# A two-layer transformer kernel: the rotary stage in batches, maxima on 32 rows with one set of keys, and five plus four maxima ahead of the first scores

## What is computed

```python
scores = einsum('bhqd,bhkd->bhqk', q, k) * 64 ** -0.5 + causal     # layer 0, head dimension 64
out = softmax(scores) @ v
...
q = rmsnorm(apply_rope(q, cos, sin), qn_w)                         # layer 1, head dimension 8
k = rmsnorm(apply_rope(k, cos, sin), kn_w)
attn = softmax(where(causal, einsum('bthd,bshd->bhts', q, k) / sqrt(8), -inf))
```

## Time and profile before

| | |
|---|---|
| runs | 1468.04 us median of 3 (1463.27 to 1469.57) |
| profiled execution, own time | 1474.87 us, span 1473.2 us |
| mean granted TensorE clock | 0.897 of full speed |
| PE busy | 1256.4 us, 85% |
| DVE busy | 982.3 us, 67% |
| ACT busy | 691.6 us, 47% |
| POOL busy | 381.6 us, 26% |
| layer 0 attention | about 39 to 590 us of the span |
| rotary stage | 925 to 960.6 us |
| layer 1 attention | 960.7 to 1276 us |

### The profile page before, as it was taken

The page is one execution under the profiler, slowest core; times in us unless marked ns, Lnnn a source line. Parts: engine busy times, 40 slices in busy tenths (PEclk is TensorE's granted clock), DMA queues, the critical chain, the costliest instruction groups (busy, mean ns, idle before and its releaser), DMA issues. The chain is left out here.

```text
span 1473.2 us, 20295 instructions
## 1 busy us (share of the span) xinstructions
PE 1256.4 (85%) x7132; PEld 758.2 (51%) x7132; DVE 982.3 (67%) x1750; ACT 691.6 (47%) x1319; POOL 381.6 (26%) x243
## 2 busy tenths in 40 slices
PE   4679999999999999589999976257988888789997
PEld 3444554545455454358888755123433343257886
DVE  4557646565755542579999956757677665448998
ACT  2232534444352434336666645213566557425664
POOL 0035465646656568000000000301111111020000
PEclk9799999999999999669999968657999979868999
DMA  3101202111120200046767400141222201111221
GB/s 107 42 15 36 50 16 60 24 50 30 39 44 16 46 16 29 4 97 148 156 147 158 96 1 0 15 115 30 49 62 61 53 20 35 29 43 60 96 90 29
DMA packets 51472, 81.54 MB, mean 55 GB/s; under 512 B 16749, under 2 KB 34453, under 8 KB 47445
## 3 DMA queue, kind: packets, MB, share of 16 engines
q1 hardware_dynamic: 51004, 79.40, 22.1%
q10 hardware_dynamic: 384, 1.05, 0.6%
HBM read 63.75 MB, written 5.68 MB: 47 GB/s over the span
## 5 line engine op out<-in xcount | busy, mean ns | idle before, releaser
L1369 PE MATMUL ps<-qA 128*128 128x512 f32 x960 | 254.1, 402 | 10.4 <-POOL qA L1479 10.4
L640 DVE TENSOR_REDUCE mraw<-ps 128x1 f32<-128x512 f32 (+3 forms) x304 | 183.2, 654 | 72.7 <-PE ps L520 41.3
L743 ACT ACTIVATE shared<-ps 128x512 f32<-128x512 f32 (+1 forms) x216 | 118.8, 565 | 227.5 <-PE ps L553 221.5
L1086 DVE TENSOR_REDUCE mraw<-ps 128x2 f32<-128x1024 f32 (+3 forms) x160 | 173.5, 1114 | 71.0 <-PE ps L994 47.8
L1141 ACT ACTIVATE shared<-ps 128x512 f32<-128x512 f32 (+2 forms) x320 | 154.7, 560 | 130.1 <-PE ps L1010 129.9
L1369 PEld LDWEIGHTS ps<-qA 128*128 128x128 f32 x960 | 183.5, 194 | 60.0 <-POOL qA L1479 12.1
L552 PE MATMUL ps<-qA,kH 128*128 128x512 f32 (+3 forms) x384 | 164.5, 438 | 8.2 <-DMA qB<-mT 6.5
L781 POOL TENSOR_TENSOR VP<-VP,shared 128x2048 f32<-128x2048 f32 (+3 forms) x40 | 129.7, 3242 | 66.1 <-ACT shared L743 64.0
L1433 ACT CAST qA<-shared 128x512 fp32r<-128x512 f32 x160 | 99.3, 620 | 87.3 <-DVE shared L1571 86.4
L1381 PE MATMUL ps<-qA,kH 128*128 128x512 f32 x480 | 135.5, 391 | 4.1 <-DVE qA L1495 4.0
L514 PE MATMUL ps<-kH,qA 128*128 128x512 f32 (+3 forms) x384 | 121.0, 380 | 17.1 <-DVE qA L630 8.9
(11 more groups left out here) (250 smaller groups left out, 1890.9 us busy)
## 6 DMA issues: line engine op xcount, KB each, us to landing
shared<-comb SPq DMA_DIRECT2D x92, 256.0 KB, 4.2
qB<-qA SPq DMA_DIRECT2D x16, 512.0 KB, 4.8
rB<-a0rec_dram SPq DMA_DIRECT2D x60, 128.0 KB, 2.9
shared<-comb SPq DMA_DIRECT2D x7, 1024.0 KB, 4.4
rB<-a1rec_dram SPq DMA_DIRECT2D x28, 128.0 KB, 2.7
e0wUp<-in_w SPq DMA_DIRECT2D x48, 64.0 KB, 4.6
qA<-q_split SPq DMA_DIRECT2D x24, 128.0 KB
q_split<-qA SPq DMA_DIRECT2D x4, 512.0 KB
```

The costliest lines, as they stand in the source:

```text
L640: nc.vector.tensor_reduce(out[:, h0:h0 + n_h, qt % 4], src, AX, ALU.max).then_inc(w_free, 1)
L743: nc.scalar.activation(probs(n)[:, hs[0]:hs[-1] + 1, lo:512], src, ACT.Exp, scale=scale)\
L1086: nc.vector.tensor_reduce(out[:, :, js[0]:js[-1] + 1, qt % 4], src, AX, ALU.max).then_inc(x_free, 1)
L1369: ins = nc.tensor.matmul(bank[0:M, :], w[par][:, at:at + M], h[:, cols], start=(r == 0), stop=(r == 2))
```

## The change

1. `stage_attention64`: the 3 projections and the first 2 maxima of qc = 1 of group 0 go ahead of unit 0, behind the first turn. 25 maxima and the turn stay in units 0 to 3.
2. `stage_attention8`: `step_of` puts 11 jobs ahead of unit 0 (first turn and then 4 maxima of qc = 1) and 22 into units 0 to 3.
3. `stage_attention8`: the maxima's matmuls read 32 rows (`TERMS`) of queries and keys, so row 32 doesn't enter. One key set is left. Masks and scores stay on 64 rows. A load has 8 transfers where it had 12, the direct loads 12 for a batch where they had 16 (`LOADS`, `DIRECT`), and two stacks less are cleared.
4. `stage_rope`: VectorE's and ScalarE's orders are written out: batch 0 goes through square, root and scaling while batch 1 is rotated between, the split of chunks 0 and 1 comes ahead of the scaling of batch 1, and ScalarE issues `direct_keys` ahead of the split of chunks 2 and 3.

```diff
-    plan = {-1: jobs_of(0, 0)}
-    spread_over(jobs_of(0, 1), 0, 4)
+    ahead = jobs_of(0, 1)
+    plan = {-1: jobs_of(0, 0) + ahead[0:U + 2]}
+    spread_over(ahead[U + 2:], 0, 4)
...
+    AHEAD = BEFORE + 4
...
-        if idx < BEFORE:
+        if idx < AHEAD:
             return -1
         if idx < EARLY:
-            return (idx - BEFORE) * 4 // (EARLY - BEFORE)
+            return (idx - AHEAD) * 4 // (EARLY - AHEAD)
...
-        DIRECT, LOADS, STORES = 16, 12, 8
+        DIRECT, LOADS, STORES = 12, 8, 8
...
-                            rows = row_tile(i, 64)
+                            rows = row_tile(i, TERMS)
                             ins = nc.tensor.matmul(pair[:, i, slot * w:(slot + 1) * w],
                                                    Q[g % 3][rows, jj, qt * P:(qt + 1) * P],
-                                                   kZero[g % 3][rows, ch * 512:ch * 512 + w],
+                                                   K[g % 3][rows, ch * 512:ch * 512 + w],
...
-                            for dst in (kZero, kOne):
-                                sp.dma_start(dst[g % 3][at:at + 2 * hd, :].bitcast(F32), src)\
-                                    .then_inc(in_ld[g % 3], 16)
+                            sp.dma_start(K[g % 3][at:at + 2 * hd, :].bitcast(F32), src).then_inc(in_ld[g % 3], 16)
...
+                first, second = rotation(0), rotation(1)
+                for _ in first:
+                    pass
+                next(second)
+                squares(0)
+                next(second)
+                scaled(0)
+                next(second)
+                lows_of(0)
+                squares(1)
+                lows_of(1)
+                scaled(1)
+                lows_of(2)
+                lows_of(3)
...
+                squared(0)
+                deviation(0)
+                highs_of(0)
+                squared(1)
+                highs_of(1)
+                deviation(1)
                 act.wait_ge(padded, 2)
                 act.wait_ge(low, 2 * CPB)
                 direct_keys(act, k, 0)
+                highs_of(2)
+                highs_of(3)
...
-                for stack in (k.kL[0], k.kL[1], k.kH[0], k.kH[1]):
+                for stack in (k.kH[0], k.kH[1]):
```

More of the change, by code:

```diff
@@ L942, in stage_attention8 @@
         LAST = slice(P - REP * hd, P)
-        Q, kZero, kOne = split_buffers(k)
+        Q, K = split_buffers(k)
         def landed(g):
@@ L1010, in score_job @@
                         ins = nc.tensor.matmul(score_bank(s)[:, slot * w:(slot + 1) * w],
-                                               kOne[g % 3][rows, kt * P:(kt + 1) * P],
+                                               K[g % 3][rows, kt * P:(kt + 1) * P],
                                                Q[g % 3][rows, h // 2, qc * 512 + lo:(qc + 1) * 512],
@@ L1154, in _ @@
                         for at in (TERMS, 64 + TERMS):
-                            ins = nc.gpsimd.memset(kOne[2][at:at + 1, :].bitcast(F32), 1.0)
+                            ins = nc.gpsimd.memset(K[2][at:at + 1, :].bitcast(F32), 1.0)
                         ins.then_inc(cleared, 1)
@@ L1700, in split_buffers @@
     Q = [k.qA[0][:, 0:2, :], k.qA[0][:, 2:4, :], k.qA[1][:, 0:2, :]]
-    kZero = [k.kL[0][:, :], k.kL[1][:, :], k.qA[1][:, 2, :]]
-    kOne = [k.kH[0][:, :], k.kH[1][:, :], k.qA[1][:, 3, :]]
-    return Q, kZero, kOne
+    K = [k.kH[0][:, :], k.kH[1][:, :], k.qA[1][:, 3, :]]
+    return Q, K
 def direct_queries(engine, k, b):
@@ L1727, in direct_keys @@
             at = 64 * i + 2 * hd * part
-            for sets in split_buffers(k)[1:]:
-                engine.dma_start(sets[b][at:at + 2 * hd, :].bitcast(F32), src).then_inc(k.a1_in[b], 16)
+            engine.dma_start(split_buffers(k)[1][b][at:at + 2 * hd, :].bitcast(F32), src).then_inc(k.a1_in[b], 16)
 def stage_rope(nc, k, qkv, sel8):
@@ L1758, in link, with rotation @@
                     dve.wait_ge(chain, n[0])
-                for b in range(B):
+                def rotation(b):
                     x = qkv[:, tiles(b), 0:HQK * hd].rearrange("p t (h e) -> p t h e", h=HQK)
@@ L1767, in _, with squares @@
                     link(nc.vector.tensor_tensor(o[:, :, :, hi], x[:, :, :, lo], sin, ALU.mult))
+                    yield
                     link(nc.vector.tensor_tensor(s[:, :, :, lo], x[:, :, :, hi], sin, ALU.mult))
+                    yield
                     link(nc.vector.tensor_tensor(s[:, :, :, hi], x[:, :, :, hi], cos, ALU.mult))
                     link(nc.vector.tensor_tensor(o[:, :, :, lo], o[:, :, :, lo], s[:, :, :, lo], ALU.subtract))
-                    roped = nc.vector.tensor_tensor(o[:, :, :, hi], o[:, :, :, hi], s[:, :, :, hi], ALU.add)
-                    roped.then_inc(rotated, 1)
-                for b in range(B):
+                    nc.vector.tensor_tensor(o[:, :, :, hi], o[:, :, :, hi], s[:, :, :, hi], ALU.add)\
+                        .then_inc(rotated, 1)
+                    yield
+                def squares(b):
                     dve.wait_ge(sq_ready, b + 1)
@@ L1778, in _, with scaled @@
                                             ALU.add).then_inc(var_ready, 1)
-                for b in range(B):
+                def scaled(b):
                     dve.wait_ge(std_ready, b + 1)
@@ L1784, in _, with lows_of @@
                                             ALU.mult).then_inc(ready, 1)
-                for ch in range(NC):
+                def lows_of(ch):
                     cols = slice(ch * 512, (ch + 1) * 512)
@@ L1799, in _, with highs_of @@
                 nc.scalar.copy(k.VP[:, :, :, 0:hd], qkv[:, :, HQK * hd:].rearrange("p t (v e) -> p t v e", v=NKV))
[L1800 to L1806, removed]
+                def highs_of(ch):
                     cols = slice(ch * 512, (ch + 1) * 512)
@@ L1811, in _, with squared, deviation @@
                                          scale=k.col("k_w")[0:32, :]).then_inc(high, 1)
+                def squared(b):
+                    act.wait_ge(rotated, b + 1)
+                    nc.scalar.activation(sq[:, tiles(b), :], r[:, tiles(b), :], ACT.Square).then_inc(sq_ready, 1)
+                def deviation(b):
+                    act.wait_ge(var_ready, b + 1)
+                    nc.scalar.activation(ms[:, 1, heads(b)], ms[:, 0, heads(b)], ACT.Sqrt).then_inc(std_ready, 1)
+                squared(0)
[4 more added lines that the diff above has]
+                deviation(1)
                 act.wait_ge(padded, 2)
```

## The result

The changed kernel takes 1544.09 us, the median of 4 runs (1541.27 to 1564.84), against 1465.72 us for the kernel before (1463.27 to 1469.57): a ratio of 1.0526, 95% interval 1.0488 to 1.0564. The forecast was 1452 in a range of 1436 to 1470. It is wrong in sign and by 92 us; not even rival A (1485) comes near.

What follows compares the result with a forecast made beforehand. VectorE and transfers were taken to bound the starts, TensorE (88% busy) layer 1's steady part; -6.5 - 6 - 4 - 2.5 - 11 + 14 = -16 us from 1468.0 gave 1452 us, range 1436 to 1470.

Steps and rivals of the forecast that it cites:

- rival A: Mode changes decide: 263 drains at 0.14 us, no overlap, more gaps lowering the clock; +17 us, 1485 us; chance 0.14.
- Part 1: Layer 0's attention: projections and maxima ahead start the first maximum 7.2 us earlier and unit 4 6.5 us earlier.
- Part 2: Rotary stage and direct loads: earlier scaling and 12 transfers for batch 0 bring layer 1's first scores 6 us earlier.
- Part 3: Layer 1's units 0 to 3: four maxima leave VectorE's chain, 4 us; a small copy avoids GpSimd's clearing, 2.5 us.
- Part 4: Layer 1's loads without the second key set: 7 us fewer TensorE waits, 4 us less lower clock, together 11 us.
- rival B: Mode changes cost nothing, 32 rows being handled as 64-row halves: -30 us, 1438 us; chance 0.15.
- Part 5: TensorE's changes between matmul shapes: 263 more at 0.093 us, plus lost overlap; price taken as 14 us, bounds 0 and 31.
- the second piece that the prediction named: On TensorE, a maximum can no longer overlap with the score in the other row half: up to 10 us more.
- The test that the prediction set itself: TensorE's group time, about 31 us: over 34 means mode changes cost more than taken, below 29 hidden or absent.

Runs made afterwards that it cites:

- the kernel on 64 rows: Changed kernel with only the maxima's matmuls put back on 64 rows, still one key set: 1433.51 us, ratio 0.9758 to the kernel before.
- the kernel with two key sets: Changed kernel with two key sets and maxima on 64 rows as before, its other edits kept: 1454.72 us, ratio 0.9906 to the kernel before.
- the kernel with 32 rows from group 3 on: Changed kernel with maxima on 64 rows up to group 2 and on 32 rows from group 3: 1498.09 us, ratio 1.0014 to the kernel before.
- all on 32 rows: Changed kernel with scores and masks cut to 32 rows like the maxima: 1535.23 us, ratio 1.0457 to the kernel before.

## Why the prediction was wrong

**Right, with sizes** (parts as the prediction numbers them). Part 1: first scores at 60.4 (59.5 forecast), unit 4 at 84.3 (85). Part 2: first maximum 33.1 us behind the start of the rotary stage (33), first scores 46.1 (47). Part 3: the copy at 0.17 us (0.2), and in the kernel with these four maxima alone 9.3 us less from the first scores to the end of group 0, rather than 6.5. Part 4: in the kernel on 64 rows `recips` waits 1.63 us at most up to 1200 us (1.7), and the waits for maxima shrink to 0.9 us. Six groups shorten by 10.7 against the kernel with two key sets, where the sum had 11. All gains together were forecast as 30 and measured as 36.0 (interval 29.5 to 41.6): that is the kernel on 64 rows, and rival B's 1438 was its time but for 5 us, though not its cause: that kernel has no changes of mode between 32 and 64 rows.

**Part 5, what a change of mode takes, was right too.** Time from the start of one pair of 512 columns to the next pair, where TensorE waits for nobody, medians (those of the changed kernel at the full clock rest on 5 to 8 places): score to maximum 0.337 us without a change (kernel on 64 rows) and 0.433 with one (changed kernel), both at the full clock: 0.096, forecast 0.093. Maximum to score 0.233 and 0.430: 0.197. That is more than the 0.096; the rest would be the second piece that the prediction named, a score that no longer overlaps with the maximum, but no run separates the two. At the lower clock score to maximum is 0.594 and 0.724. Such rows of the changed kernel at the full clock:

```profile
1230.59 0.51 PE L1012 MATMUL ps<-qA 64*128 64x512 f32 x2
1231.03 0.49 PE L985 MATMUL ps<-kH,qA 32*128 32x512 f32 x2
1231.45 0.88 PE L1012 MATMUL ps<-qA 64*128 64x512 f32 x2
```

and at the lower:

```profile
1152.75 0.79 PE L1012 MATMUL ps<-qA,kH 64*128 64x512 f32 x2
1153.48 0.80 PE L985 MATMUL ps<-kH,qA 32*128 32x512 f32 x2
1154.20 0.88 PE L1012 MATMUL ps<-qA,kH 64*128 64x512 f32 x2
```

Most of it is hidden: the group between 1131.8 and 1163.5 us of the kernel with 32 rows from group 3 on, wholly at 1.00, takes 31.7 us, a group on 64 rows 30.4 (182.7 / 6). That is 1.3 a group, or 2.0 against the same group on 64 rows (29.7): some 10 to 16 for eight, where 14 was taken, from a single group. At 0.50 it is 3.8 a group (49.7, the mean of the changed kernel's groups 1 to 3, against 45.9 all on 32 rows).

**The step that failed** is the sum's silent term: the prediction let the clock follow the idle time of TensorE alone. Under part 4 it took 4 us off because fewer gaps would mean less time at 0.50, and under part 5 it charged a 32-row matmul its late start and its lost overlap, and nothing for how the clock would take fewer rows. At 1.00 all 8 groups would have cost some 10 to 16 us more than on 64 rows, an estimate of 1444 to 1450 us for the whole. The other 94 to 100 are the clock: a group takes 46 us all on 32 rows at 0.50 where it takes 30.4 on 64 rows at 1.00, and the changed kernel spent 325 of the 373 us from 960 to 1333 at 0.50. Rival A had the lower clock as a result of more gaps; there were fewer gaps. Nor does a run show the drain of 0.14 us at each change that this rival counts with; measured is the later start, 0.096 us from score to maximum and 0.197 from maximum to score at the full clock. In the 110 us from 1090 on TensorE idles 1.9, in the 182.7 of the 64-row kernel 18.9, and it is the first that stays at 0.50.

The test that the prediction set itself pointed the right way and named the wrong cause: groups of over 34 us were to mean that changes of mode cost more. Four of the six took 49 to 51, with each change at the price taken.

The clock didn't follow TensorE's busy share: it is busy 237.6 of 246.7 us at 0.50 in the changed kernel and 163.8 of 182.7 at 0.99 with maxima on 64 rows. In these kernels the clock went by how many rows the matmuls read as well.

**Open.** How the level depends on rows between 33, 48 and 64, on columns, and why scores and maxima on 32 rows don't weigh quite alike. What starts a fall is open too: some come behind a turn's idle time and some behind none, and no kernel moved the turns.

## What to carry to other kernels

A matmul that reads fewer rows wasn't cheaper on TensorE here (0.427 us from a maximum to the next score at 0.50, all on 32 rows or all on 64), and where such matmuls filled much of the time the engine stayed at half its clock for 247 us on end while it looked 96% busy. Before cutting the rows of a matmul, ask what the granted clock will make of it, and keep the rows filled up with zeros if they cost no time. Read the granted clock beside the busy share in every stretch: a "busier" TensorE after a change may be a slower one. Measure such an edit with each row count by itself: here everything else in the change gave 36 us, and the 32 in one line took 110.

## What the runs showed of the hardware

- With more rows of zeros the clock was higher: 64 rows (31 of them zero) 1433.5 us and 0.99 in the six groups, 48 rows 1507.9 and 0.59, 33 rows 1540.9 and 0.50, with the same useful work but for the masks' terms.
- The same code ran with two courses of the clock: the ten runs of the kernel with 32 rows from group 3 on fell in two bundles 32 to 53 us apart, with mean granted clocks of 0.884 to 0.898 and 0.848 to 0.854 (only the faster bundle was profiled). A median of few runs of such a kernel says little.
- The full clock ended while TensorE hardly waited: all on 32 rows after 13.7 us at 1.00 with no wait over 0.9 us, while on 64 rows it outlasted three idle times of 1.6 to 1.7 us.
- A change between 64-row and 32-row matmuls cost 0.096 us from score to maximum at the full clock, 0.13 at the lower (0.724 less 0.594), and 0.197 from maximum to score at the full clock.
